# A shorter front and node numbers moved from GpSimd copies to 4-byte DMAs in a two-layer graph network on one core

## What is computed

```python
h = relu(layernorm(x))
# layer 0: graph convolution, dst is the receiving node
deg = segment_sum(1, dst); dinv = rsqrt(deg)
out = segment_sum((h @ W_lin @ W_gcn)[src] * (dinv[src] * dinv[dst])[:, None], dst) + b_gcn
x = x + relu(layernorm(out) * gamma + beta)
# layer 1: attention over edges, src is the segment
h = relu(layernorm(x)); q = h @ Wq + bq
k = edge_attr @ Wk + bk; v = edge_attr_n2 @ Wv + bv
score = (q[src] * k summed per head) * scale
attn = softmax of score over the edges of one src
x = x + segment_sum(v * attn, src) @ Wo + bo
```

## Time and profile before

| | |
|---|---|
| median of 3 runs | 3288.93 us (3287.18 to 3289.5) |
| the profiled execution, its own time | 3284.15 us |
| its span in the profile | 3282.4 us |
| busy: PE, DVE, ACT, POOL | 2659.5, 2409.7, 1868.0, 2122.8 us |
| mean granted TensorE clock | 0.895 of full speed |

### The profile page before, as it was taken

How to read it: one execution, slowest core, us unless ns; L and a number is a source line. 1 busy time by engine, 2 the same in 40 slices (tenths; PEclk the granted TensorE clock), 3 DMA queues, 4 the chain that set the end, 5 groups by cost and what they waited for, 6 DMA issues and landing times.

```text
span 3282.4 us, 63589 instructions
## 1 busy us (share of the span) xinstructions
PE 2659.5 (81%) x20446; PEld 1943.1 (59%) x20446; DVE 2409.7 (73%) x4642; ACT 1868.0 (57%) x6125; POOL 2122.8 (65%) x2014
## 2 busy tenths in 40 slices
PE   3446765988888887885670499999999999999988
PEld 2114442555555554553340388888888887888878
DVE  7799998999998888986960255555555556888876
ACT  0234447888887777873550255555555555666653
POOL 2388887888888888888877688888888881000000
PEclk9556666999999999997675799999999999999999
DMA  3255453555555555556896899999999997777751
GB/s 93 88 184 180 166 182 115 167 176 167 176 170 179 170 183 169 179 172 203 271 299 218 283 363 360 362 369 361 360 358 359 360 363 239 222 222 223 222 173 39
DMA packets 407231, 750.45 MB, mean 229 GB/s; under 512 B 47610, under 2 KB 283214, under 8 KB 406906
## 3 DMA queue, kind: packets, MB, share of 16 engines
q1 hardware_dynamic: 277866, 438.42, 42.0%
q0 software_dynamic: 96160, 291.60, 23.9%
q10 hardware_dynamic: 32880, 16.39, 1.7%
HBM read 500.16 MB, written 246.06 MB: 227 GB/s over the span
## 4 chain that ended last, share of the span: by engine, by line
PE 56%; POOL 19%; DVE 8%; issue 8%; ACT 4%; DMA 1%; DVEq 0%; POOLq 0%; SPq 0%; ACTq 0%
POOL table_s L575 18%; PE bank L1579 12%; PE bank L1606 12%; PE bank L1588 7%; PE bank L1597 6%; PE bank L1005 6%; PE bank L900 4%; PE bank L1573 3%; PE bank L986 3%; DVE parts L809 3%; ACT work L690 2%; PE bank L947 1%; POOL ring L563 1%; PE bank L1956 1%; DVE row_base L749 1%
## 5 line engine op out<-in xcount | busy, mean ns | idle before, releaser
L575 POOL DMA_INDIRECT table_s<-ring,place x1612 | 1854.8, 1151 | 481.5 <-issue 442.5
L651 ACT ACTIVATE row_base<-row_base 128x196 f32<-128x196 f32 x1414 | 495.8, 355 | 215.1 <-DVE row_base L745 215.1
L1682 DVE TENSOR_REDUCE gmax<-bank 128x1 f32<-128x384 f32 (+1 forms) x400 | 301.4, 753 | 279.8 <-PE bank L1579 270.4
L1641 ACT COPY exT<-bank 128x384 f32<-128x384 f32 x596 | 268.0, 483 | 404.6 <-PE bank L1597 400.7
L1579 PE MATMUL bank<-kT,G 128*128 128x512 f32 (+2 forms) x1192 | 472.9, 505 | 0.3 <-ACT kT L1634 0.3
L1606 PE MATMUL bank<-kv_rows,exT 128*128 128x129 f32 x3576 | 465.8, 275 | 0.1
L1634 ACT COPY kT<-bank 128x384 f32<-128x384 f32 x596 | 274.9, 485 | 288.0 <-PE bank L1588 286.3
L1606 PEld LDWEIGHTS bank<-kv_rows,exT 128*128 128x128 f32 x3576 | 431.5, 192 | 0.5 <-issue 0.5
L690 ACT CAST work<-bank 128x392 bf16<-128x392 f32 x784 | 353.5, 501 | 136.7 <-PE bank L986 125.0
L1005 PE MATMUL bank<-parts,work 128*128 128x384 bf16 x2401 | 429.6, 330 | 0.0
L1588 PE MATMUL bank<-ident,kv_rows 128*128 128x128 f32 x1788 | 298.2, 279 | 137.7 <-DMA kv_rows<-table_s 137.2
(11 more groups left out here) (301 smaller groups left out, 3944.8 us busy)
## 6 DMA issues: line engine op xcount, KB each, us to landing
kv_rows<-table_s SPq DMA_DIRECT2D x196, 816.0 KB
ring<-in_kv SPq DMA_DIRECT2D x278, 512.0 KB
kv_rows<-table_s SPq DMA_DIRECT2D x204, 408.0 KB, 4.0
ring<-in_kv POOLq DMA_DIRECT2D x124, 512.0 KB
table_s<-ring,place POOLq DMA_INDIRECT x1612
G<-G_dram SPq DMA_DIRECT2D x400, 64.0 KB
G_dram<-gst ACTq DMA_DIRECT2D x50, 256.0 KB, 4.4
x_dram<-xres ACTq DMA_DIRECT2D x5, 640.0 KB, 5.2
```

Of the source, the lines that this page charges most:

```text
L575: pool.indirect_dma_start(out=m["table_s"], out_offset=bass.IndirectOffsetOnAxis(ap=m["place"][0:n, i, k:k + 1], axis=0), in_=m["ring"][0: ...
L651: last = nc.scalar.activation(at, at, ACT.Identity, accum_out=m["place_f"][:, i % 2, h * STREAMS // 2 + k:h * STREAMS // 2 + k + 1])
L1682: dve.tensor_reduce(gmax, of_scores(n), AX_X, ALU.max).then_inc(m["reduced"], 1)
```

## The change

- The one-hot comparisons of the front take 16-bit columns in pairs (`in_pairs`), `his` and `los` become f16 pairs, and HIS becomes 14, so that it is even. The rulers `iota_l` and `ruler` are made by GpSimd directly, first of all constants; the copies of them on ScalarE go, and the large iota `ruler_w` goes behind the last signal. VectorE starts when src has landed.
- TensorE counts first, then prepares the weights, then sums the spread (`spread_sums`).
- The bases of the second part (`second_rows`) are made after the ranking of step 0; `hot(0)` (`tile_hots`) moves into the front.
- The node numbers of steps 0 to 138 are written into `ring` by `load_numbers`, a DMA of 4-byte elements on SyncE, in place of the copies on GpSimd; the count that `scatter_rows` waits for grows from 32 to 48. From step 139 on the copies stay.
- Key batches 0 to 2 are gathered after scatter step 31.
- POOL_STEPS becomes (114, 136).

```diff
-HIS, LOS = 13, 16
+HIS, LOS = 14, 16
-POOL_STEPS = (110, 136)
+POOL_STEPS = (114, 136)
@@ load
-    sp.wait_ge(m["paddings"], 1)
-    for t, k, shift, loaded in (src, next):
+    for turn, (t, k, shift, loaded) in enumerate((src, next)):
+        sp.wait_ge(m["paddings"], turn + 1)
@@ constants
-    for t in (m["raw"]["src"], m["raw"]["dst"], m["next"]):
+    pool.memset(m["raw"]["src"][:, :], PAD_KEY).then_inc(m["paddings"], 1)
+    for t in ("iota_l", "ruler"):
+        last = pool.iota(m[t][:, :], [[1, m[t].shape[1]]], base=0, channel_multiplier=0, allow_small_or_imprecise_dtypes=True)
+    last.then_inc(m["consts"], 1)
+    for t in (m["raw"]["dst"], m["next"]):
...
-    pool.iota(m["ruler_w"] ...)
     ... .then_inc(m["consts"], 1)
+    pool.iota(m["ruler_w"] ...)
@@ source_counts
-    c(dve.tensor_copy(m["his"], whole))
+    for w in range(2):
+        last = dve.tensor_copy(m["his"][:, :, w], whole)
+    c(last)
...
-    c(dve.tensor_reduce(m["delta"] ...))
     for q in range(STREAMS):
-        dve.tensor_tensor(m["hot_hi"][k][:, 0:n, :], column(m["his"][:, first:first + n], [P, n, HIS]),
-                          row_of(m["iota_n"][:, 0:HIS], [P, n, HIS]), ALU.is_equal)
-        dve.tensor_tensor(m["hot_lo"] ...)
+        for hot_n, key, wide in (("hot_hi", "his", HIS), ("hot_lo", "los", LOS)):
+            last = dve.tensor_tensor(m[hot_n][k][:, 0:n, :].rearrange("p c (l w) -> p c l w", w=2),
+                                     m["iota_l"][:, 0:wide].rearrange("p (a l w) -> p a l w", a=1, w=2).to_broadcast([P, n, wide // 2, 2]),
+                                     in_pairs(m[key][:, first:first + n, :], wide), ALU.is_equal)
+        last.then_inc(m["src_hot"], 1)
+    dve.wait_ge(m["consts"], 2)
+    c(dve.tensor_reduce(m["delta"] ...))
...
+    tile_hots(m, dve, 0)
     dve.wait_ge(m["src_counted"], 1)
-    (bases of both parts, second_row)
+    part_base(m, dve, c, 0).then_inc(m["row_base_ready"], 1)
+def second_rows(m, dve, c):
+    c(part_base(m, dve, c, 1))
+    (second_row).then_inc(m["row_base_ready"], 1)
+    dve.wait_ge(m["row_base_ready"], 2)
@@ front_block, TensorE
-            pe.wait_ge(m["consts"], 1)
-            prepare_weights(nc, m, pe)
             count_sources(nc, m, pe)
+            pe.wait_ge(m["consts"], 2)
+            prepare_weights(nc, m, pe)
+            spread_sums(nc, m, pe)
+def load_numbers(m, sp, i):
+    u, first = i % KRING, STREAMS - columns(i)
+    sp.dma_start(m["ring"][:, u, first:STREAMS, KEY_AT:KEY_AT + 1], m["sources"][:, i, first:STREAMS].rearrange("p (s a) -> p s a", a=1),
+                 allow_slow_non_contiguous=True).then_inc(m["rows_loaded"][u], 16)
@@ scatter_rows
-    for j in ((0, 1) if i == 0 else (i + 1,) if i + 1 < STEPS else ()):
+    for j in (i + 1,) if LATE <= i + 1 < STEPS else ():
-        pool.wait_ge(m["rows_loaded"][u], 32 * (i // KRING + 1))
+        pool.wait_ge(m["rows_loaded"][u], 48 * (i // KRING + 1))
-    pool.wait_ge(m["keys_ready"], i + 1)
+        pool.wait_ge(m["keys_ready"], i - LATE + 1)      # from LATE on
@@ scatter_stage
-        gathers.setdefault(sent_by(max(FIRST_HOT - 4, key_step(b) - 13)), []).append(b)
+        gathers.setdefault(sent_by(max(FIRST_HOT, key_step(b) - 13)), []).append(b)
             load_rows(m, sp, i, m["rows_loaded"])
+            if i == 0:
+                sp.wait_ge(m["ones_ready"], 1)
+            load_numbers(m, sp, i)
-        hot(0)
         for i in range(STEPS):
             rank(i)
+            if i == 0:
+                second_rows(m, dve, c)
@@ nodes_stage: load_numbers beside load_rows on SyncE; VectorE and ScalarE
-        dve.wait_ge(m["keys_ready"], SHIFT_STEPS)
+        for u in range(KRING):
+            dve.wait_ge(m["rows_loaded"][u], 48 * (SHIFT_STEPS // KRING + 1))
```

## The result

The changed kernel takes 3215.47 us, the median of 4 runs (3214.52 to 3218.16), against 3288.97 us before (4 runs): the ratio is 0.9779, with a 95% interval from 0.9764 to 0.9793. That is 73.5 us less, where 98.5 less were forecast (3190, range 3166 to 3238). The profiled execution took 3214.52 us, its span is 3212.8.

A forecast was written before the change was run, and what follows sets the result against it. The prediction took the bound to be the front, then GpSimd's chain of 136 scatter steps, then an untouched layer 1. Front -45.1 and steps -53.4 sum to -98.5 us: 3190 us forecast, range 3166 to 3238.

The forecast's parts named there:

- terms 1 to 6: Front before the first scatter: earlier start, casts, comparisons, weights, spread and second bases together gain 45.1 us, first scatter at 87.2.
- Term 4: Front: TensorE's weights work hides behind the counts at no cost, as the constants are done early; uncovered it costs 7 us.
- Term 7: Scatter steps: each copy gone from GpSimd saves 0.39 us, its waiting included, 53 us over 136 steps (bounds 9 and 53).
- Rival A: Scatter steps: the copies' waiting moves into the scatters, 44 us of the gain are lost, 3234 us; chance 0.13.
- Term 8: Gathers 0 to 2 moved from step 29 to 31: GpSimd's wait for starts falls to about 5 us, gain 4.9.
- Term 9: second_rows on VectorE between the ranking of steps 0 and 1 makes GpSimd wait 1.5 us (0 to 8.3).
- Term 10: Node numbers by DMA: about 28 ns a 4-byte packet, no bottleneck in the ranking, 3 us lost in the nodes stage.
- rival B: Scatter steps: the 4-byte packets make the DMA engines the bound, 3570 us at 150 ns a packet; chance 0.07.
- Term 11: POOL_STEPS from 110 to 114: SyncE's held-back load becomes that of step 117, costed at nothing.
- Rival C: Front: denser counting lifts TensorE's clock and the spread product halves, 6 us more gain, 3184 us; chance 0.12.
- Rival D: Loads come late in places (start, nodes stage), 25 us in all, 3215 us; chance 0.06.

The follow-up runs named there:

- copies_new_front: The changed kernel with the node numbers of all steps copied by GpSimd again and no DMAs for them: 3232.39 us.
- no_numbers: The changed kernel without the node-number DMAs and without the copies they replace up to step 138, so layer 1 works on wrong numbers: 3215.37 us.
- numbers_only: The kernel before with only the copies replaced by the 4-byte DMAs, front, POOL_STEPS and gathers as before: 3273.53 us against 3291.15.
- copies_in_two: The changed kernel with the copies back on GpSimd, each made in two halves one right behind the other: 3272.91 us.
- gathers_29: The changed kernel with key batches 0 to 2 gathered after scatter step 29 again: 3239.66 us.
- busy_21_rows_3: The changed kernel plus 21 unread TensorE products before the spread product, second part's bases moved after the ranking of step 3: 3208.4 us beside 3215.56.
- no_two_inputs: The changed kernel with each edge block's two 16-bit comparisons replaced by single-input sums about as long, making first-layer sums meaningless: 3122.46 us.

## Why the prediction was right in sign and 25 us too good

- **Front** (terms 1 to 6): right, -45.0 for -45.1. VectorE starts at 6.75 (7.0); the casts cost 2.2 (2.1); the comparisons end after 27.1 us (26.3), since a pair takes 3.38 to 3.55 us, not 3.29; from the last count to the spread product 8.7 (8.3 before), as the weights hid in it; the product 12.29, 0.83 more (0.9); from its end to the first scatter 7.8 less (8.3). That the sum meets the forecast within 0.1 us is in part luck: the comparisons lost 0.8 us, and the last stream's counts, at full clock, gave 1.2 back that no term had. Term 4's cover was thin, too: the constants came at 47.9, when VectorE had waited 0.71 us for them and 1.3 us before TensorE came to its weights. I had taken them to be done as early as before.
- **Term 7** is the step that failed: "the scatters that stand between the copies meet VectorE as often as before". They don't. Above the unheld durations (0.968, 0.209 and 0.96 us for scatter, copy and gather, 0.32 for a pair of halves), GpSimd was held for 270 us in the stage before, 261 after; 270 in copies_new_front, 258 to 261 in no_numbers and numbers_only, 298 in copies_in_two. Taking the copies away removed 10 of the 44 us that they were held. What holds is, for the most part, VectorE's two-input instructions, which stay as many, and a chain that always runs meets them about as often with whatever stands there. So a copy was worth its own 0.21 us, less the 0.14 of the boundary, plus some 0.07 of holding: 0.14, as measured, or 19 of the 53 us. Rival A was the right mechanism, with 34 of its 44 us. The time lies in the forecast range because the range had been drawn wide enough for A, to which the prediction gave a chance of 0.13.
- **Term 8**: right in kind, too small. The wait left was 0.4 us, not 5: gain 9.1 (4.9). In the new kernel the move is worth 24 us (gathers_29, with 23.2 us of wait; the prediction had put that wait at about 30).
- **Term 9**: 1.86 us (1.5). The 8.3 us of waiting for places in the earlier trace rows, which I counted in the steps, were nearly all (7.37) the wait of the first scatter. The groups there add up to 1712, and to 1704 only without it; it enters no term.
- **Term 10**: 7 ns a packet, not 28, and no loss in the nodes stage (3 forecast). The row at 15 to 16 us was of weights loaded from device memory, with 238 of 623 packets of 512 B or more. The DMA share in the ranking rose from 0.52 to 0.57; rival B is out.
- **Term 11**: no wait, as forecast. It gained 5 us over (110, 136), and these are less holding (261 us for 266) and no wait for rows, so they may well be the stage's own play, below.
- **Rival C**: half right. The counting did lift the clock, by its durations: TensorE's 34 pairs fell from 3.19 to 1.94 us. Only those of the last stream stand on the path, 1.2 us; the 6 us in front of the spread product lost the clock again. By the rule of the Trainium skill that the prediction cites (TensorE: Matmul & The Clock Gate, Part 1: The HAM clock gate) an array kept busy has full clock; with the gap filled it had. **Rival D**: no load came late.

By the terms the steps are: copies -19 to -22, gathers -9.1 + 2.6, places +2.5, which is -23 to -26 for the measured -25.9. What stays open is the stage's own play: kernels whose GpSimd does the same work took 1676 to 1687 us for it, and the times of one kernel differ by up to 10.9 us (busy_21_rows_3). That it comes from how the two engines' instructions happen to meet is likely, but not shown. An edit of under 7 us can't be judged here by one profile.

## What to carry to other kernels

When an engine is held by another one's instructions, the holding belongs to the holder: removing a held instruction saves its unheld duration, read where the holder stands still, and little of the rest. To get the rest, change the holder's instructions: sums with a single input in place of the edge comparisons took 112 us of holding away (no_two_inputs), and products with an input in PSUM held nothing. Don't count on a single input alone, as casts held scatters too. And when a chain gets shorter at its head, look at every point where it meets data from elsewhere: moving the gathers by two steps was worth 24 us, all copies together 19.

## What the hardware showed that I had not expected

- A scatter of GpSimd is held by a 16-bit comparison of VectorE at one moment, about 0.13 us behind its start (415 of 433), and not at its end (0 of 171); casts and integer instructions with one input held four scatters at their end. One scatter of 0.97 us took 5.01 us.
- 4-byte packets within SBUF took about 7 ns each of a DMA engine (an estimate, from 8320 of them in 100 us).
- GpSimd's affine selects are held too: 1.67 us in place of 0.90 for 128x128 numbers.
- Filling 6 us of TensorE's idle time with useless products halved the next 12.3 us of fp32 products (6.18 and 6.28 us).
